# A decoder layer on one core: experts in twelve tiles of 256 rows and eight of 128, one normalisation pass, three weight buffers, and the first quad's weights loaded in quarters

## What is computed

```
aff = feats @ centroids.T
eid = argmax(aff, axis=1)                       # one expert for each row
xhat = (feats - mean(feats)) * rsqrt(var(feats) + EPS)
for e in range(8):
    h = xhat * gamma[e] + beta[e]
    y = feats + relu(h @ w1[e] + b1[e]) @ w2[e] + b2[e]
    alpha = sigmoid(feats @ centroids[e])
    out += (eid == e) * (alpha * y + (1 - alpha) * feats)
```

## Time and profile before

| | |
|---|---|
| median of three executions | 1551.66 us |
| the profiled execution's own time | 1550.12 us |
| its span, first to last instruction | 1548.4 us |
| TensorE busy, share of the span | 1428.6 us, 92% |
| mean granted TensorE clock | 0.975 of full |
| self-attention, cross-attention, experts: ends at about | 649, 1234, 1548 us |

### The profile page before, as it was taken

The page is one execution under the profiler, slowest core; times in us unless marked ns, Lnnn a source line. Parts: engine busy times, 40 slices in busy tenths (PEclk is TensorE's granted clock), DMA queues, the critical chain, the costliest instruction groups (busy, mean ns, idle before and its releaser), DMA issues.

```text
span 1548.4 us, 40200 instructions
## 1 busy us (share of the span) xinstructions
PE 1428.6 (92%) x12305; PEld 1237.3 (80%) x12305; DVE 971.0 (63%) x2495; ACT 764.9 (49%) x1879; POOL 672.1 (43%) x1021
## 2 busy tenths in 40 slices
PE   4999999999999999679999999999999469999997
PEld 3888888888888888668888888888888358888886
DVE  5747474747474747256777777777776445555553
ACT  4747464747474747225666656556565212222221
POOL 5434344434343444512355554554554423333332
PEclk9999999999999999879999999999999779999999
DMA  5606151616161616266776777677666144555451
GB/s 187 140 9 152 37 141 45 142 44 149 38 151 35 149 38 157 53 187 189 189 197 184 185 198 189 177 193 195 176 186 201 50 163 164 173 199 182 152 187 55
DMA packets 181963, 218.30 MB, mean 141 GB/s; under 512 B 83838, under 2 KB 150309, under 8 KB 181638
## 3 DMA queue, kind: packets, MB, share of 16 engines
q1 hardware_dynamic: 176360, 208.56, 49.5%
q0 software_dynamic: 3968, 6.59, 1.3%
q10 hardware_dynamic: 1568, 2.30, 0.5%
HBM read 138.67 MB, written 80.48 MB: 142 GB/s over the span
## 4 chain that ended last, share of the span: by engine, by line
PE 50%; DVE 3%; DMA 2%; issue 2%; POOL 1%; SPq 1%; ACT 0%; DVEq 0%; ACTq 0%; POOLq 0%
PE psd_h L2199 9%; PE psd_y L2207 9%; PE psb_s L1707 6%; PE psb_t L1717 5%; PE psb_o L1730 4%; PE psb_p L55 3%; PE psb_p L56 3%; PE psb_p L57 3%; PE psb_p L1670 2%; PE psb_f L1753 2%; DVE row_max L1459 1%; PE psb_f L1738 1%; DMA k<-packed_keys 1%; PE psb_p L1765 1%; PE psd_x L2179 1%
## 5 line engine op out<-in xcount | busy, mean ns | idle before, releaser
L1459 DVE TENSOR_REDUCE row_max<-psb_s 100x1 f32<-100x361 f32 x512 | 265.6, 531 | 140.8 <-PE psb_s L1707 135.8
L1333 ACT ACTIVATE probs<-psb_t 121x400 f32<-121x400 f32 (+1 forms) x384 | 190.5, 508 | 87.7 <-PE psb_t L1717 81.7
L1707 PE MATMUL psb_s<-k,q 97*100 97x362 f32 x512 | 184.8, 363 | 13.9 <-DMA k<-packed_keys 5.1
L522 POOL TENSOR_TENSOR diag<-neg_ident,row_max 100x400 fp32r<-100x400 f32 x128 | 113.0, 904 | 175.2 <-DVE row_max L615 146.5
L1717 PE MATMUL psb_t<-q,k 98*121 98x200 f32 (+1 forms) x768 | 147.0, 273 | 2.0 <-ACT probs L1333 2.0
L2199 PE MATMUL psd_h<-h_in,w_sb 128*128 128x256 f32 x640 | 143.4, 383 | 1.4 <-ACT h_in L2065 1.4
L2207 PE MATMUL psd_y<-w_sb,hid 128*128 128x256 f32 x640 | 144.5, 379 | 0.0
L2199 PEld LDWEIGHTS psd_h<-h_in,w_sb 128*128 128x128 f32 x640 | 122.9, 192 | 18.8 <-issue 1.8
L2207 PEld LDWEIGHTS psd_y<-w_sb,hid 128*128 128x128 f32 x640 | 120.1, 190 | 15.5
L1717 PEld LDWEIGHTS psb_t<-q,k 98*121 98x121 f32 (+1 forms) x768 | 125.3, 184 | 5.4 <-ACT probs L1333 2.7
L2080 ACT ACTIVATE hid<-psd_h,b_sb 128x256 f32<-128x256 f32 x100 | 47.4, 474 | 147.8 <-PE psd_h L2199 146.6
(11 more groups left out here) (236 smaller groups left out, 3700.5 us busy)
## 6 DMA issues: line engine op xcount, KB each, us to landing
w_sb<-in_w SPq DMA_DIRECT2D x40, 1024.0 KB, 7.5
routed_rows<-empty SPq DMA_DIRECT2D x7, 3855.0 KB, 19.6
packed_keys<-k_st SPq DMA_DIRECT2D x32, 724.0 KB, 4.3
k<-packed_keys SPq DMA_DIRECT2D x64, 362.0 KB
v_rows<-v_tok SPq DMA_DIRECT2D x32, 400.0 KB
v_ext<-v_rows SPq DMA_DIRECT2D x32, 400.0 KB
q<-packed_queries SPq DMA_DIRECT2D x64, 200.0 KB
k<-packed_keys SPq DMA_DIRECT2D x64, 181.0 KB
```

The lines of the kernel that those rows point to most:

```text
L522: pool.tensor_tensor(diag[:, g % 2], c.neg_ident[0:S, 0:S].unsqueeze(1).to_broadcast([S, GH, S]), row_max[:, g // 2 % 2, g % 2].unsqueeze( ...
L1333: act.activation(probs[0:KT[kt], u % 2, kt], ps_t[i % 2][0:KT[kt], 0:4 * S], ACT.Exp, scale=HD2 ** -0.5).then_inc(probs_ready, 1)
L1459: dve.reduce_max(row_max[:, p, h:h + 1], ps_s[h % 2][0:S, 0:S2], AX_X).then_inc(max_ready, 1)
L1707: pe.matmul(ps_s[h % 2][0:S, 0:S2E], q2[0:97, p, u, g, S * a:S * (a + 1)], k2[0:97, p, u, g], start=True, stop=True).then_inc(scores_ready, 1)
```

## The change

1. **Tiles.** Experts has twelve tiles of 256 rows, then eight of 128, 20 in all; every loop is written out. The table of tiles is worked out twice, once for each kind. Every tile still loads its expert's 2 MB of weights.
2. **One pass.** DVE takes one set of moments. From the variance v POOL makes two roots, of v(1+EPS)+EPS*EPS for `xhat` and of v+EPS for `feats`, and DVE normalises to both from the rows.
3. **Three weight and three row buffers.** Weights and rows of tile j+2 are asked for when tile j-1 has left TensorE.
4. **POOL's order.** Roots of tile j+1, the scatter of tile j-1, then `xf` of tile j+1. In small tiles TensorE turns the next tile's rows in the middle of the w2 matmuls. There are three PSUM buffers for y.
5. **First quad.** SP issues x and then wqkT in four pieces of 0.5 MB, on one queue. DVE's low parts come after the normalisation, one of them before the split of x and three behind it. TensorE waits for each piece where it first needs it. POOL splits the other weights by halves.

```diff
-T = 256
-TILES = (B * S + E * (T - 1)) // T
+UNIT = 128
+T = 2 * UNIT
+BIG = B * S // T
+SMALL = (B * S + E * (UNIT - 1)) // UNIT - 2 * BIG
+TILES = BIG + SMALL
+PATTERN = (2,) * BIG + (1,) * SMALL
+HALVES = PATTERN
...
             load_x(0, x_first)
-            sp.wait_ge(w_loaded[0], 16)
+            for n, (qk, half) in enumerate(PIECES):
+                first = O1 * qk + O1 // 2 * half
+                sp.dma_start(columns(w_stage, qk, half), wqkT[:, first:first + O1 // 2].rearrange(
+                    "(k p) n -> p k n", p=128)).then_inc(piece_loaded[n], 16)
             load_x(1, x_second)
             for i, w in ((2, wvT), (3, woT)):
-                sp.wait_ge(w_lo_ready, i - 1)
+                sp.wait_ge(w_lo_ready, i + 1)
...
+            high_bits(0)
+            high_bits(1)
             leading_bits(0)
+            high_bits(2)
+            high_bits(3)
...
             trailing_bits(0)
+            for n in range(1, len(PIECES)):
+                low_bits(n)
...
+def halves_until(j, step=1):
+
+    return sum(HALVES[j % step:max(j, 0):step])
...
+            load_rows(sp, c, 1, xs)
+            sp.wait_ge(c.tiles_ready, 4)
+            for j in range(TILES - 2):
+                reach(sp, xf_ready, j)
+                reach(sp, token_ready, j)
+                load_rows(sp, c, j + 2, xs)
+                reach(sp, y_filled, halves_until(j))
+                load_weights(sp, c, j + 2, w1_sb[(j + 2) % 3], w2_sb[(j + 2) % 3], w1, w2)
...
+            for j in range(TILES):
+                if j + 1 < TILES:
+                    roots(j + 1)
+                if j > 0:
+                    finish(j - 1)
+                if j + 1 < TILES:
+                    residual(j + 1)
+            finish(TILES - 1)
...
+                dve.tensor_reduce(z[:, 0:nh], prod[:, 0:nh], AX_X, ALU.add).then_inc(z_ready, 1)
+                reach(dve, scattered[j % 2], 16 * halves_until(j, 2))
+                dve.tensor_copy(token[:, j % 2, 0:nh], rows[:, j % 3, 0:nh, D]).then_inc(token_ready, 1)
+                dve.wait_ge(ez_ready, j + 1)
...
                     for k in range(KD):
-                        ins = pe.matmul(ps_h[f % 4][:, 0:T], c.w1_sb[:, p, k, 128 * f:128 * (f + 1)], h_in[:, p, k],
-                                        start=(k == 0), stop=(k == KD - 1))
+                        ins = pe.matmul(ps_h[f % 4][:, 0:UNIT * nh], w1_sb[j % 3][:, k, 128 * f:128 * (f + 1)],
+                                        h_in[:, j % 2, k, 0:UNIT * nh], start=(k == 0), stop=(k == KD - 1))
                     ins.then_inc(hid_filled, 1)
-                reach(pe, y_ready, NH * j)
-                for t in range(NH):
+                for t in range(nh):
+                    n = halves_until(j) + t
+                    reach(pe, y_ready, n - 2)
                     for f in range(NF):
                         if t == 0:
                             copied(j, f)
+                        if f == 4 and nh == 1 and j + 1 < TILES:
+                            turn(j + 1)
```

More of the change, by code:

```diff
@@ L1558, in tiles, with count, running @@
-                link(dve.tensor_reduce(first_f, past_n, AX_X, ALU.add))
+                def count(dst, kind):
+                    link(dve.tensor_tensor(full, total.unsqueeze(2).to_broadcast([1, E, MAXT]),
+                                           steps[:, kind].unsqueeze(1).to_broadcast([1, E, MAXT]), ALU.is_gt))
+                    link(dve.tensor_reduce(dst, full, AX_X, ALU.add))
+                def running(dst, src):
+                    link(dve.tensor_tensor(both, upto[:], src.unsqueeze(1).to_broadcast([1, E, E]), ALU.mult))
+                    link(dve.tensor_reduce(dst, both, AX_X, ALU.add))
@@ L2039, in finish, with residual @@
+            def residual(j):
+                nh = HALVES[j]
+                pool.wait_ge(normalised, 2 * j + 2)
+                reach(pool, res_ready, halves_until(j - 1))
+                pool.tensor_tensor(xf[:, j % 2, 0:nh], rows[:, j % 3, 0:nh, 0:D], feats[:, 0:nh], ALU.add
+                                   ).then_inc(xf_ready, 1)
+            def finish(j):
+                for t in range(HALVES[j]):
+                    pool.wait_ge(res_ready, halves_until(j) + t + 1)
                     pool.sem_inc(pool_passed, 1)
@@ L2053, in _ @@
-            for p in range(2):
-                pool.wait_ge(scattered[p], 16 * NH * (TILES // 2))
+                        out=out, out_offset=bass.IndirectOffsetOnAxis(ap=token[:, j % 2, t:t + 1], axis=0),
+                        in_=res[:, j % 2, t, :], in_offset=None, bounds_check=B * S - 1,
+                        oob_is_err=False).then_inc(scattered[j % 2], 16)
+            roots(0)
+            residual(0)
+            for j in range(TILES):
[5 more added lines that the diff above has]
+                    residual(j + 1)
@@ L2068, in prepare @@
                 act.wait_ge(z_ready, j + 1)
-                act.activation(ez[:], z[:], ACT.Exp, scale=-1.0).then_inc(ez_ready, 1)
-            prepare(0, 0)
-            def step(j, p, last):
-                e = expert_of(act, c, j)
+                act.activation(ez[:, 0:nh], z[:, 0:nh], ACT.Exp, scale=-1.0).then_inc(ez_ready, 1)
+            prepare(0)
+            for j in range(TILES):
+                nh, e = HALVES[j], expert_of(act, c, j)
                 for f in HID_ACT:
@@ L2138, in _, with moments @@
-            features(0, 0)
-            again(0, 0)
-            center(0, 0)
-            weigh(0, 0)
-            def step(j, p, last):
-                e = expert_of(dve, c, j)
+            def moments(j):
+                dve.wait_ge(rows_loaded[j % 3], 16 * (j // 3 + 1))
+                for t in range(HALVES[j]):
+                    dve.bn_stats(stats[:, t], rows[:, j % 3, t, 0:D]).then_inc(moment_steps, 1)
+                dve.wait_ge(moment_steps, halves_until(j) + halves_until(j + 1))
+                dve.sem_inc(dve_passed, 1)
+                for t in range(HALVES[j]):
+                    dve.bn_aggr(mv[:, t], stats[:, t]).then_inc(moment_steps, 1)
@@ L2145, in step @@
+            moments(0)
+            normalize(0)
+            weigh(0)
+            for j in range(TILES):
+                nh, e = HALVES[j], expert_of(dve, c, j)
                 for f in HID_DVE:
@@ L2147, in step @@
                     if f == 1:
[L2148 to L2156 removed]
+                        reach(dve, y_filled, halves_until(j))
@@ L2170, in _ @@
-            over_tiles(dve, step)
+                reach(dve, scattered[j % 2], 16 * halves_until(j, 2))
+                for t in range(nh):
+                    n = halves_until(j) + t
+                    dve.wait_ge(y_filled, n + 1)
+                    dve.tensor_tensor(y[:, t], ps_y[n % 3][:, 0:D], c.b2_sb[:, bass.ds(e, 1), :].rearrange(
+                        "p o d -> p (o d)"), ALU.add).then_inc(y_ready, 1)
+                for t in range(nh):
+                    dve.wait_ge(y_ready, halves_until(j) + t + 1)
+                    dve.scalar_tensor_tensor(out=res[:, j % 2, t], in0=y[:, t], scalar=alpha[:, j % 2, t:t + 1],
+                                             in1=xf[:, j % 2, t], op0=ALU.mult, op1=ALU.add).then_inc(res_ready, 1)
@@ L2188, in copied @@
                     pe.wait_ge(hid_dve, len(HID_DVE) * j + HID_DVE.index(f) + 1)
-            turn(0, 0)
-            def step(j, p, last):
-                pe.wait_ge(c.w_loaded[p], (j - p) * 16 + 32)
+            turn(0)
+            for j in range(TILES):
+                nh = HALVES[j]
+                pe.wait_ge(c.w_loaded[j % 3], 32 * (j // 3 + 1))
                 pe.wait_ge(h_in_ready, j + 1)
@@ L2237, in build @@
         c.xs_cleared = ctx.enter_context(nc.semaphore("xs_cleared"))
+        c.scattered = [ctx.enter_context(nc.semaphore(f"scattered{p}")) for p in range(2)]
         c.act_passed = ctx.enter_context(nc.semaphore("act_passed"))
```

397 lines of the change are left out of this document (186 added, 211 removed).

## The result

The changed kernel takes **1495.26 us**, the median of 4 runs (1494.93 to 1496.70), beside 1552.45 us for the kernel before on the same chip. The ratio is 0.9633, with a 95% interval from 0.9617 to 0.9650: 57 us less. The forecast was 1491 us in a range of 1480 to 1513. Here the profiled execution is the slowest of the four, 1496.7 us with a span of 1494.8 us, so the two profiled spans are 53.6 us apart.

The account below looks back on a forecast made before the run. TensorE, busy 92%, was taken to bound the kernel. From 1550.1 us, tiles -47.5, normalisation -2.7, table -0.5, end -1.3 and first quad -8.0 gave 1490.1; the median was forecast at 1491 us, range 1480 to 1513.

Parts of the forecast that it names:

- The large tiles: Experts stage: large tiles stay 14.25 us apart, bound by TensorE; eight fewer save 114.0 us.
- The small tile's own need: Small expert tiles: TensorE needs 7.23 us each, with w1 records taken as 0.11 us apart.
- The rival by which loads don't overlap matmuls: Small tiles: w1 at 0.216 us a record, 3.4 us more a tile, 1509 us in all; chance 3%.
- The scatter's wait: Small tiles: DVE's tokens wait for a scatter, stalling TensorE 2.4 us before its sixth filling, so tiles alternate 7.5 and 9.8.
- Landing when the load ends: Experts: a scatter issued amid a load of weights lands at that load's end, about 8.2 us into a small tile.
- The sum for the eight tiles: Eight small expert tiles: 4 x 7.5 + 3 x 9.8 + 7.1 = 66.5 us, 8.7 more than 8 x 7.23.
- a rival of 10%: Small tiles: TensorE's clock falls to 1.2 GHz, giving 1540 us throughout or 1515 for half of them; chance 10%.
- The hand-over: Tile 0, from rows' landing to first turn: one normalisation pass saves 2.7 us, the turn coming 3.8 us after its rows.
- the table: Ahead of the experts: 14 linked DVE operations in place of 18 before SP may start, saving 0.5 us.
- The end: Last tile: one scatter in place of two issued 1.28 us apart, saving 1.3 us.
- The first quad: Kernel start: x lands at 8.0 us, ahead of the weights; 8.0 us saved in all, bounds 5 and 9.5.
- the threshold of 3.0 us a tile: Experts, slower-than-before rival: late instructions decide it from 59.6/20 = 3.0 us per tile; 1571 us at 4; chance 3%.

## Why the prediction was right, and where it was off

- **The large tiles** stayed at 14.25 us, and 114 us went for eight of them: right.
- **The small tile's own need**, 7.23 us from records 0.11 apart, is right: tile 12 took 7.25, and the narrower w1 shows that 100 and 128 columns cost the same. The rival by which loads don't overlap matmuls is out.
- **The scatter's wait** was the right mechanism, with the right place (ahead of the sixth filling, released by DVE's filling 1). Its sum was a little low: three stalls of 2.4 us, 7.2, for four of 3.71, 2.41, 1.02 and 2.07, 9.2. That long and short tiles would alternate held only roughly, and no stall but one had the size forecast. "Landing when the load ends" holds: DVE got the tokens that wait for the second scatter of tile 11 at 1423.90, when the DMA engines' share had dropped to 0.61 between two loads, and in the stretch in which the next wait ended the DMA engines came to rest (columns as in the earlier trace rows):

```profile
1443.00:1444.00 1.00, 1.00 (x11) 1.00 (x11) 0.00 (x0) 0.37 (x1) 0.00 (x0) 1.00 0.82 262
1444.00:1445.00 1.00, 0.87 (x8) 0.68 (x7) 0.38 (x3) 0.37 (x1) 0.00 (x0) 1.00 0.14 25
```

  DVE's token follows at 1444.43. Without loads a scatter took 2.3 us, and issued earlier under one it took 2.4 longer. This agrees with the Trainium skill, DMA: Bandwidth & Descriptors, Queues, rings and completion order, by which a semaphore write lands only after every earlier write of its DMA engine. But the runs don't tell a late semaphore write from bytes that merely share the engines with the load. What I had not seen is that the worst stall is in the first pair: tile 11 is large and sends two scatters 1.5 us apart through the same wait. Nor was the load alone to blame, as the two runs without loads show.
- **The sum for the eight tiles was 66.5 us and came to 73.7.** The term that failed is what a stall costs: I priced it by its length and left the clock to a rival of 10% that had it low through half or all of the tiles. In fact two stalls brought it down for some 7 and 3 us, which cost 4.3 us in all, and one put back alone cost 5.9 us for a wait of 3.3 more. A second, smaller miss: in tiles without a wait I took DVE to be in time. It is not quite, since `y` and `res` stand ahead of filling 1, and this costs some 0.36 us a tile; with the stalls' edges 2.6 in all. The forecast sum had 1.7 of it, in the 7.5 and 9.8 us of its tiles, for which it gives no row. So the 7.2 us that were missing are 4.3 of clock, 2.0 of stalls and 0.9 of this rest.
- **The hand-over**: the turn came 3.8 us after the rows, 2.7 sooner, both as forecast. With the table 3.5 us were gained between the first quad and tile 0, forecast 3.2; as the code ahead varies by more, only the 2.7 are shown.
- **The end** gained 2.0 us in the trace where I had 1.3. The last scatter's issue came 0.9 us sooner behind the last matmul (2.1 for 3.0), and 1.0 lies behind that issue, for which the forecast had no term and the runs no reason.
- **The first quad**: x at 8.5 us (forecast 8.0), the first matmul 7.9 us sooner (forecast 8.0). That this came so close is partly luck: x was 5.1 us sooner for 5.7 forecast, and the way from x to the matmul 2.8 shorter for 2.3. POOL's addition took 0.24 us again. No wait for the value weights took its place: POOL had the two halves ready at 26.7 and 30.2 us (forecast 25 and 28.5), and TensorE waits for neither between 24 and 45 us.
- **The sum** was 1490.1 us against the profiled execution, which took 1496.7. Of these 6.6 the tiles are 7.2 and the first quad 0.1, less 0.3 at the hand-over and 0.7 at the end: 6.3; another 0.2 lie outside the span. That the rest fits to 0.1 us is luck, with a stretch of the kernel in between that differs by several us from run to run. A slip that changes nothing: the threshold of 3.0 us a tile is worked out from 59.6 us, for which no row stands; the forecast's savings add up to 60.0.

## What to carry to other kernels

When tiles shrink, list what does not shrink with them: a wait for a transfer, and small vector steps queued in front of what the bound engine needs next. A ring of buffers that had 2 us to spare in a 14 us tile ran dry in a 7 us one; one more buffer of results and tokens took 11 us off here, issuing the transfer earlier only 3. And price a stall of TensorE not by its length alone: look at the granted clock behind it.

## What the runs showed of the hardware that was not expected

- **A stall's length doesn't say whether the clock falls.** Stalls of 3.27, 3.71 and 3.76 us brought it down, but so did one of 2.07 and one of 2.18, while 2.41 us in the changed kernel, 2.67 and 2.73 with the fillings given out anew and two buffers, and seven stalls of up to 2.3 with the early scatter did not. What decides it is open.
- **128x128 weights with 100 or 128 moving columns take the same 0.11 us a record**; with 256 it is 0.216.
- **The same code in the middle of the kernel varies by up to 7.6 us between profiled runs.** From the first matmul of the split to the first of w1 in tile 0, the kernels that differ from each other only ahead of or behind that stretch took from 1222.2 us (first stage as before) to 1229.8 (no loads and early scatter); the changed kernel took 1225.1. The granted clock at the end of cross-attention goes along with it only in part. It was 0.95 in the changed kernel and 0.88 with fewer columns (1227.4 us; columns as in the earlier trace rows), but it was 0.95 without loads as well, which took 1228.2:

```profile
1124.00:1224.00 100.00, 85.73 (x1044) 72.38 (x1043) 65.28 (x207) 51.19 (x140) 50.91 (x109) 0.95 0.48 134
```

```profile
1124.00:1224.00 100.00, 88.47 (x1005) 75.12 (x1003) 62.21 (x192) 49.58 (x136) 49.71 (x108) 0.88 0.45 127
```

  Why it differs is open. It is the reason why edits worth 1 to 3 us were read here from the traces, stretch by stretch, and not from the medians.
